# Squaring the expert activations on GpSimd instead of ScalarE in a fused attention and expert kernel

## The chip, the cores and the metric

The kernel runs on one core of a Trainium2 chip. The core's engines are PE (TensorE, matrix products and transposes), DVE (VectorE), ACT (ScalarE), POOL (GpSimd) and SP (SyncE, here only DMA). Each has its own instruction queue, works through it in order, and waits on semaphores that the others raise. The metric is the device time in microseconds of one execution; lower is better.

## The reference

The input is 2048 rows of 256 numbers, all float32. After a layer norm two layers read the same rows, and their outputs are added to x. The first has windowed attention and a fast-weight memory that goes from chunk to chunk (128 rows). The second is a mixture of 32 experts, of which 8 count for each row, and a shared expert. The change touches the experts; the memory matters because the rest of each chunk waits for it.

```python
def relu2(x): return jnp.square(jax.nn.relu(x))
x_lat = x @ fc1_w.T                                   # 128 wide
h = relu2(jnp.einsum('tl,eil->eti', x_lat, w1))       # 32 experts of 128
h = h * cw.T[:, :, None]
y_lat = jnp.einsum('eti,eli->tl', h, w2)
routed = y_lat @ fc2_w.T
shared = relu2(x @ shared_up_w.T) @ shared_down_w.T
...
# memory, per chunk, for each of W0, W1, W2 of four heads
for a, b, c in NS_COEFFS:                             # five steps
    A = X @ X.transpose(0, 2, 1)
    B = b * A + c * (A @ A)
    X = a * X + B @ X
W = (W + X) / (norm_of_rows(W + X) + 1e-05) * n
```

## The kernel before, in words

There are 16 chunks of 128 rows. `body(i, last)` is one round and is written out once per engine. A round finishes chunk i and prepares chunk m = i + 1. Fifteen rounds are alike and the last is shorter, since nothing follows. The order on each engine is written by hand: the five Newton-Schulz steps have four stages each (stages 0 to 19), for two groups g of heads whose buffers carry the group's number, and `fill` says what else stands behind each stage.

A stage of the memory goes as follows. PE transposes X (`ns_turn`), ACT copies the result to XT (`xt`), PE forms the gram products (`ns_gram`), DVE copies them to Am (`ns_a`), PE squares Am (`ns_pair`), DVE forms Mp (`ns_m`), PE multiplies by X, and DVE adds aX (`ns_x`), which POOL has computed from X and a_tile (`ax`). After the last step DVE updates Wn, sums its rows, POOL takes the roots (`row_pow`), DVE scales Wn (`renorm`), PE transposes it (`turn_w`) and ACT copies it to WT (`w_T`). Then comes the k side of the next round: products of WT on PE, copies `ks` on ACT, products kt, hid, dhb and dga on DVE with one (`k_u`) on POOL, and the gradients on PE (`grads`). A gradient norm follows, whose powers are on POOL (`ss_pow`).

The experts are done in eight blocks of four (u = 0 to 7). `h_up` on PE writes one 128x512 block to the PSUM bank HB. `h_relu` on ACT copies it with a relu into one of four buffers hq, then squares that buffer in place. `y_down` on PE reads hq and writes the bank YB. `y_acc` on DVE (or `y_first` on ACT for block 0) scales it by the routing weight and adds it into acc. HB is free again when the relu is done. Blocks 0 and 1 of a chunk are computed at the end of the round before. `shared_sq` on POOL squares the shared expert's block, of the same size, once a round.

In each round ACT's squares stand in its queue at these places: block 0 before the copy yT, 1 before the WT copies, 2 before the shared relu, 3 before the first XT copies, 4 before the copies of the query output, 5 before the sigmoids sgs, the third pair of XT copies and the square sq of the q and k heads, 6 before a table load, 7 before a logarithm and the copy prT.

Of the kernel before, what the change touches and what calls it, by code (L numbers as in the profile page):

```python
# [27 lines left out]
ALU = mybir.AluOpType  # L28
ACT = mybir.ActivationFunctionType
# [3 lines left out]
P = 128  # L33
# [12 lines left out]
EU = 4  # L46
NU = E // EU
# [26 lines left out]
def build(nc, x, wall_d, rows_d, wo, fast_d, affine_d, fc1T, fc2T, e1T, e2T, upT, downT, ident_d, fixed_d, out):  # L74
# [3 lines left out]
    with ExitStack() as ctx:  # L78
        def sb(name, shape):
            return ctx.enter_context(nc.sbuf_tensor(name, shape, F32))  # L80

        def bank(name):
            return ctx.enter_context(nc.psum_tensor(name, [P, 512], F32))

        def sem(name):
            return ctx.enter_context(nc.semaphore(name))
# [9 lines left out]
        e2_s = sb("e2_s", [P, E, P])  # L96
# [89 lines left out]
        xlT = sb("xlT", [P, P])  # L186
        ur = sb("ur", [P, SC, P])
        us = sb("us", [P, SC, P])
        hq = [sb(f"hq{b}", [P, EU, P]) for b in range(4)]
        acc = sb("acc", [P, EU, P])  # L190
        ya = sb("ya", [P, 2, P])
        ys = sb("ys", [P, P])
# [8 lines left out]
        HB = bank("HB")  # L201
        YB = bank("YB")
# [29 lines left out]
        e_h, e_hr, e_hq, e_y, e_acc = (sem(n) for n in ("h", "h_relu", "h_sq", "y", "acc"))  # L232
# [41 lines left out]
        @block.gpsimd  # L274
        def _(pool):

            win_scores = Expect(pool, e_as, "win_scores", first=2)
            win_pv = Expect(pool, e_av, "win_pv", first=2)
            win_raw = Expect(pool, e_rawv, "win_raw", first=3)
            win_vw = Expect(pool, e_win, "win_vw", first=5, step=2)  # L280
            pool.wait_ge(e_init, 1)

            def power(dst, src, expo, n):
                return pool.tensor_tensor(dst, src, expo[:, 0:n], ALU.pow)  # L284

            def prep_rstd(m):
                pool.wait_ge(e_veps, m + 1)
                power(rstd[:, 0:1], rstd[:, 1:2], neghalf, 1).then_inc(e_rstd, 1)

            def prep_n8(m):  # L290
                pool.wait_ge(e_ss8, m + 1)
                power(r8[:, 1, :], r8[:, 0, :], half, 8).then_inc(e_n8, 1)

            def prep_kl(m):

                pool.wait_ge(e_lr, m + 1)
                for g in range(G):
                    pool.wait_ge(e_dw[g], m)
                kk = qkn[:, D:2 * D].rearrange("p (h c) -> p h c", c=HD)
                vv = sl[:, 2 * D:3 * D].rearrange("p (h c) -> p h c", c=HD)  # L300
                for dst, src, n in ((kl0, kk, 0), (kl2, kk, 2), (vl1, vv, 1)):
                    ins = pool.tensor_tensor(dst[:, :, :], src, lr[:, :, n:n + 1].to_broadcast([P, NH, HD]), ALU.mult)
                ins.then_inc(e_kl, 1)

            def window(m, known):

                if known:
                    pool.wait_ge(e_as, m)
                    pool.wait_ge(e_av, m)
                    pool.wait_ge(e_rawv, m + 1)  # L310
                else:
                    win_scores.wait()
                    win_pv.wait()
                    win_raw.wait()
                pool.tensor_copy(akT[:, :, 0, :], akT[:, :, 1, :])
                pool.tensor_copy(vw[:, 0, :], vw[:, 1, :]).then_inc(e_win, 1)

                if known:
                    pool.wait_ge(e_win, 2 * m + 1)
                else:  # L320
                    win_vw.wait()
                pool.tensor_copy(vw[:, 1, :], raw[:, 2 * D:3 * D]).then_inc(e_win, 1)

            def restore_mask():

                pool.wait_ge(e_sm, 1)
                pool.wait_ge(e_later, 16 * NLATER)
                pool.tensor_copy(mask[:, 0, :], mask_prev[:, :]).then_inc(e_mask, 1)

            def k_u(i, g):  # L330
                pool.wait_ge(e_kc[g], i + 1)
                pool.tensor_tensor(kt[g][:, 3, :], ks[g][:, 1, :], ks[g][:, 2, :], ALU.mult).then_inc(e_ku[g], 1)

            def ss_pow(i, g):
                pool.wait_ge(e_sst[g], 3 * i + 1)
                power(r3[g][:, 2, :], r3[g][:, 1, :], half, 3).then_inc(e_pw[g], 1)

            def ax(i, g, it):
                pool.wait_ge(e_x[g], (NI + 1) * i + it + 1)
                pool.tensor_tensor(aX[g][:, :, :].rearrange("p w c -> p (w c)"),  # L340
                                   X[g][:, :, :].rearrange("p w c -> p (w c)"), a_tile[:, it, :],
                                   ALU.mult).then_inc(e_ax[g], 1)

            def row_pow(m, g):

                pool.wait_ge(e_rn[g], m + 1)
                power(r3[g][:, 4, :], r3[g][:, 3, :], half, 3).then_inc(e_rp[g], 1)

            def rms_pow(i):
                pool.wait_ge(e_msq, 2 * i + 2)  # L350
                power(r4[:, 1, :], r4[:, 0, :], neghalf, 4).then_inc(e_rms, 1)

            def shared_sq(i):
                pool.wait_ge(e_ur, i + 1)
                pool.tensor_tensor(us[:, :, :], ur[:, :, :], ur[:, :, :], ALU.mult).then_inc(e_us, 1)

            def body(i, last):
                if last:
                    shared_sq(i)
                    rms_pow(i)  # L360
                    return
                m = i + 1
                first = i == 0
                k_u(i, 0)
                k_u(i, 1)
                for g in range(G):
                    ss_pow(i, g)
                prep_rstd(m)
                fill = {0: [lambda: shared_sq(i)], 3: [lambda: rms_pow(i)],
                        9: [lambda: prep_n8(m)], 16: [lambda: window(m, first)],  # L370
                        17: [lambda: prep_kl(m)]}
                if first:
                    fill[13] = [restore_mask]
                for st in range(4 * NI):
                    if st % 4 == 0:
                        for g in range(G):
                            ax(i, g, st // 4)
                    for f in fill.get(st, []):
                        f()
                for g in range(G):  # L380
                    row_pow(m, g)

            prep_rstd(0)
            for g in range(G):
                row_pow(0, g)
            prep_n8(0)
            window(0, True)
            prep_kl(0)

            body(0, False)  # L390
            for i in range(1, LAST):
                body(i, False)
            body(LAST, True)


        @block.scalar
        def _(act):
# [9 lines left out]
            def a(out_, in_, func, **kw):  # L407
                return nc.scalar.activation(out_, in_, func, **kw)  # L408
# [78 lines left out]
                a(ur[:, :, :].rearrange("p s t -> p (s t)"), M0[:, :], ACT.Relu).then_inc(e_ur, 1)  # L487

            def h_relu(i, u):
                n = NU * i + u  # L490
                flat = hq[n % 4][:, :, :].rearrange("p s t -> p (s t)")
                act.wait_ge(e_h, n + 1)
                if n >= 4:
                    act.wait_ge(e_y, n - 3)
                a(flat, HB[:, :], ACT.Relu).then_inc(e_hr, 1)
                act.wait_ge(e_hr, n + 1)
                a(flat, flat, ACT.Square).then_inc(e_hq, 1)

            def y_first(i):

# [102 lines left out]
        def _(pe):  # L603
# [10 lines left out]
            def mm(out_, lhsT, rhs, start=True, stop=True):  # L614
                return pe.matmul(out_, lhsT, rhs, start=start, stop=stop)  # L615
# [203 lines left out]
            def y_down(i, u):  # L819
                pe.wait_ge(e_hq, NU * i + u + 1)  # L820
                pe.wait_ge(e_acc, NU * i + u)
                for e in range(EU):
                    ins = mm(YB[:, e * P:(e + 1) * P], hq[(NU * i + u) % 4][:, e, :], e2_s[:, EU * u + e, :])
                ins.then_inc(e_y, 1)

            def turn_y(i, last):
# [127 lines left out]
        def _(dve):  # L954
# [165 lines left out]
            def ns_m(i, g, it):  # L1120

                _, b, c = NS[it]
                dve.wait_ge(e_prod[g], 3 * NI * i + 3 * it + 2)
                nc.vector.scalar_tensor_tensor(Mp[g][:, :, :].rearrange("p w c -> p (w c)"),  # L1124
                                               Am[g][:, :, :].rearrange("p w c -> p (w c)"), b / c, CA[g][:, 0:3 * HD],
                                               ALU.mult, ALU.add).then_inc(e_mp[g], 1)
# [313 lines left out]
```

## Time and profile before

| | |
|---|---|
| median of three runs | 824.2 us (823.67 to 824.67) |
| the profiled execution | 823.67 us |
| its span, first to last instruction | 821.6 us |
| granted TensorE clock, mean | 0.996 of full speed |
| busy: PE, DVE, ACT, POOL | 773.3, 658.4, 429.5, 276.4 us |
| squares on ACT | 128, of 630 ns |
| aX products on POOL | 150, of 658 ns |

The profile gives, for each engine, the time in which its instructions ran. Matrix products are pipelined, so that a busy PE isn't PE at its peak. The idle time of an engine counts only where another one, or the end, depends on it; the waits and the timeline show that. Weight loads (PEld) overlap the products.

### The profile page before, as it was taken

Reading aid. Unit: us, or ns where it says so; the run is one execution under the profiler, and the core shown is the slowest. Engines: PE = TensorE matmul, PEld = TensorE weight load, DVE = VectorE, ACT = ScalarE, POOL = GpSimd, SP = SyncE. Lnnn points to the kernel's source line nnn. Section 1 sums busy time; section 2 is a strip of 40 time slices with the busy share of each in tenths; the row PEclk is TensorE's granted clock in tenths of the full one; section 3 lists DMA queues with packets and bytes.
Section 4 is the critical chain, followed back from the end, with each engine's and each line's share of the span. In section 5 each row is a group of like instructions: output and inputs, shape, how many; then the busy total and the mean of one; then the engine's idle time right before and its main releaser. Section 6 shows DMA issues by size and latency. Waiting matters only on the chain.

```text
span 821.6 us, 24761 instructions
## 1 busy us (share of the span) xinstructions
PE 773.3 (94%) x9776; PEld 668.8 (81%) x9776; DVE 658.4 (80%) x2592; ACT 429.5 (52%) x996; POOL 276.4 (34%) x407
## 2 busy tenths in 40 slices
PE   3899999999999999999999999999999999999997
PEld 1878888788887888878888788887888888788886
DVE  4778788887878879888698886978879788797865
ACT  2655455454555545555545555455555554545544
POOL 1433333334333343333433334333343323433220
PEclk9899999999999999999999999999999999999999
DMA  8100000000000000000000000000000000000000
GB/s 322 57 2 15 8 2 21 3 14 8 2 21 2 14 9 2 21 2 15 8 3 20 2 15 8 3 21 2 15 8 2 21 2 15 8 2 15 2 15 7
DMA packets 9810, 15.08 MB, mean 18 GB/s; under 512 B 1120, under 2 KB 8928, under 8 KB 9440
## 3 DMA queue, kind: packets, MB, share of 16 engines
q1 hardware_dynamic: 7904, 7.80, 3.1%
q10 hardware_dynamic: 1792, 5.70, 1.8%
q8 instruction: 78, 1.28, 0.7%
q14 instruction: 36, 0.29, 0.1%
HBM read 11.41 MB, written 2.10 MB: 16 GB/s over the span
## 4 chain that ended last, share of the span: by engine, by line
PE 75%; ACT 15%; DVE 5%; issue 4%; DMA 1%; SPq 0%; DVEq 0%
PE CC L615 24%; PE M L615 21%; PE HB L615 13%; PE YB L615 10%; ACT hq L408 6%; DVE acc L1314 2%; ACT L556 2%; ACT XT L408 2%; DVE Am L1117 2%; DMA rows<-in_rows 1%; PE M L773 1%; ACT prT L408 1%; ACT WT L408 1%; ACT sq L408 1%; PE CC L686 1%
## 5 line engine op out<-in xcount | busy, mean ns | idle before, releaser
L340 POOL TENSOR_TENSOR aX<-X,a_tile 128x192 f32<-128x192 f32 x150 | 95.6, 658 | 177.0 <-DVE X L1132 177.0
L615 PE MATMUL YB<-e_s,hq 128*128 128x128 f32 x1024 | 141.2, 281 | 5.9 <-DVE acc L1314 5.9
L615 PE MATMUL HB<-xlT,e_s 128*128 128x128 f32 x1024 | 142.9, 283 | 0.4 <-ACT xlT L408 0.4
L408 ACT ACTIVATE hq<-HB 128x512 f32<-128x512 f32 x128 | 76.4, 597 | 121.5 <-PE HB L615 121.5
L1314 DVE SCALAR_TENSOR_TENSOR acc<-YB,cw,acc 128x128 f32<-128x128 f32 x448 | 125.5, 342 | 15.0 <-PE YB L615 15.0
L284 POOL TENSOR_TENSOR r<-r,half 128x3 f32<-128x3 f32 (+1 forms) x78 | 77.9, 1011 | 171.9 <-DVE r L1102 71.3
L615 PEld LDWEIGHTS YB<-e_s,hq 128*128 128x128 f32 x1024 | 124.2, 191 | 11.7 <-issue 8.5
L615 PEld LDWEIGHTS HB<-xlT,e_s 128*128 128x128 f32 x1024 | 126.6, 193 | 6.9 <-ACT xlT L408 0.7
L408 ACT ACTIVATE hq<-hq 128x512 f32<-128x512 f32 x128 | 80.7, 630 | 4.0
L615 PEld LDWEIGHTS CC<-Am 64*64 64x64 f32 x1800 | 60.3, 134 | 20.6 <-DVE Am L1117 15.2
L615 PE MATMUL CC<-Am 64*64 64x64 f32 x1800 | 72.6, 222 | 1.8
L408 ACT ACTIVATE XT<-CC 128x256 f32<-128x256 f32 x150 | 48.7, 376 | 46.3 <-PE CC L686 46.1
L615 PEld LDWEIGHTS CC<-X,Mp 64*64 64x64 f32 x1800 | 58.3, 134 | 15.5 <-issue 9.0
L615 PE MATMUL CC<-X,Mp 64*64 64x64 f32 x1800 | 68.6, 222 | 0.0
L1132 DVE SCALAR_TENSOR_TENSOR X<-CC,aX 128x192 f32<-128x192 f32 x150 | 51.2, 350 | 20.7 <-PE CC L615 20.6
L1117 DVE COPY Am<-CC 128x192 f32<-128x192 f32 x150 | 48.6, 349 | 22.2 <-PE CC L615 20.6
L615 PEld LDWEIGHTS CC<-XT 64*64 64x64 f32 x1800 | 43.2, 133 | 28.1 <-ACT XT L408 26.0
L615 PE MATMUL CC<-XT 64*64 64x64 f32 x1800 | 55.5, 232 | 5.7 <-ACT XT L408 5.7
L615 PE MATMUL M<-wall,xnT 128*128 128x512 f32 (+1 forms) x128 | 56.7, 549 | 3.6 <-DMA rows<-in_rows 3.6
L1124 DVE SCALAR_TENSOR_TENSOR Mp<-Am,CC 128x192 f32<-128x192 f32 x150 | 49.8, 349 | 5.3 <-PE CC L615 4.8
L408 ACT ACTIVATE sig<-M 128x512 f32<-128x512 f32 (+1 forms) x32 | 15.7, 490 | 53.9 <-PE M L615 53.8
L284 POOL TENSOR_TENSOR r<-r,neghalf 128x4 f32<-128x4 f32 x16 | 16.2, 1015 | 71.6 <-DVE r L1187 71.6
(180 smaller groups left out, 1487.8 us busy)
## 6 DMA issues: line engine op xcount, KB each, us to landing
xa<-in_x SPq DMA_DIRECT2D x16, 128.0 KB, 2.1
e_s<-in_e1T ACTq DMA_DIRECT2D x1, 2048.0 KB, 12.8
e_s<-in_e2T ACTq DMA_DIRECT2D x1, 2048.0 KB, 19.5
xr<-in_x SPq DMA_DIRECT2D x16, 128.0 KB, 2.2
out<-ot SPq DMA_DIRECT2D x16, 128.0 KB, 1.7
wall<-in_wall SPq DMA_DIRECT2D x1, 820.0 KB, 7.0
up_s<-in_upT ACTq DMA_DIRECT2D x1, 512.0 KB, 15.5
down_s<-in_downT ACTq DMA_DIRECT2D x1, 512.0 KB, 19.5
```

The lines of the kernel that those rows point to most:

```text
L284: return pool.tensor_tensor(dst, src, expo[:, 0:n], ALU.pow)
L340: pool.tensor_tensor(aX[g][:, :, :].rearrange("p w c -> p (w c)"), X[g][:, :, :].rearrange("p w c -> p (w c)"), a_tile[:, it, :], ALU.mult ...
L408: return nc.scalar.activation(out_, in_, func, **kw)
L556: act.preload_act_table_set("sigmoid_and_others")
L615: return pe.matmul(out_, lhsT, rhs, start=start, stop=stop)
L686: pe.transpose(CA[g][:, P:2 * P], X[g][:, 1:3, :].rearrange("p w c -> p (w c)"), ident[:, :])\
L773: ins = pe.transpose(M1[:, n * P:(n + 1) * P], pr[:, h, w, :], ident[:, :])
L1117: nc.vector.tensor_copy(Am[g][:, :, :], CC[g][:, 0:6 * P].rearrange("p (w c) -> p w c", w=3)[:, :, 0:HD])\
L1124: nc.vector.scalar_tensor_tensor(Mp[g][:, :, :].rearrange("p w c -> p (w c)"), Am[g][:, :, :].rearrange("p w c -> p (w c)"), b / c, CA[g][ ...
L1132: nc.vector.scalar_tensor_tensor(X[g][:, :, :].rearrange("p w c -> p (w c)"), CB[g][:, 0:3 * HD], NS[it][2], aX[g][:, :, :].rearrange("p w ...
L1314: ins = nc.vector.scalar_tensor_tensor(acc[:, e, :], y, w, acc[:, e, :], ALU.mult, ALU.add)
```

## The change

The two halves of `h_relu` are taken apart. ACT only does the relu, from HB into one of two new buffers hr. POOL does the square as a product of hr with itself, into one of two buffers hq (four before). The POOL instruction `h_sq(i, u)` waits for the relu of its block and for `y_down` of the block two before it; the relu waits for the square of the block two before it. `h_sq` is put into POOL's queue at eight places of a round.

```diff
-        hq = [sb(f"hq{b}", [P, EU, P]) for b in range(4)]
+        hr = [sb(f"hr{b}", [P, EU, P]) for b in range(2)]
+        hq = [sb(f"hq{b}", [P, EU, P]) for b in range(2)]
...
+            def h_sq(i, u):
+                pool.wait_ge(e_hr, NU * i + u + 1)
+                if u > 1 or not (isinstance(i, int) and i == 0):
+                    pool.wait_ge(e_y, NU * i + u - 1)
+                b = u % 2
+                pool.tensor_tensor(hq[b][:, :, :], hr[b][:, :, :], hr[b][:, :, :], ALU.mult).then_inc(e_hq, 1)
...
             def h_relu(i, u):
-                n = NU * i + u
-                flat = hq[n % 4][:, :, :].rearrange("p s t -> p (s t)")
-                act.wait_ge(e_h, n + 1)
-                if n >= 4:
-                    act.wait_ge(e_y, n - 3)
-                a(flat, HB[:, :], ACT.Relu).then_inc(e_hr, 1)
-                act.wait_ge(e_hr, n + 1)
-                a(flat, flat, ACT.Square).then_inc(e_hq, 1)
+                act.wait_ge(e_h, NU * i + u + 1)
+                if u > 1 or not (isinstance(i, int) and i == 0):
+                    act.wait_ge(e_hq, NU * i + u - 1)
+                a(hr[u % 2][:, :, :].rearrange("p s t -> p (s t)"), HB[:, :], ACT.Relu).then_inc(e_hr, 1)
...
-                    ins = mm(YB[:, e * P:(e + 1) * P], hq[(NU * i + u) % 4][:, e, :], e2_s[:, EU * u + e, :])
+                    ins = mm(YB[:, e * P:(e + 1) * P], hq[u % 2][:, e, :], e2_s[:, EU * u + e, :])
```

On POOL, from the roots of the row sums at a round's end (r30, r31 with half) to the first aX of the next round, before:

```order
L284 TENSOR_TENSOR r30<-r30,half 128x3
L284 TENSOR_TENSOR r31<-r31,half 128x3
L332 TENSOR_TENSOR kt0<-ks0 128x128
L332 TENSOR_TENSOR kt1<-ks1 128x128
L284 TENSOR_TENSOR r30<-r30,half 128x3
L284 TENSOR_TENSOR r31<-r31,half 128x3
L284 TENSOR_TENSOR rstd<-rstd,neghalf 128x1
L340 TENSOR_TENSOR aX0<-X0,a_tile 128x192
```

and with the change:

```order
L285 TENSOR_TENSOR r31<-r31,half 128x3
L363 TENSOR_TENSOR hq0<-hr0 128x512
L333 TENSOR_TENSOR kt0<-ks0 128x128
L333 TENSOR_TENSOR kt1<-ks1 128x128
L363 TENSOR_TENSOR hq1<-hr1 128x512
L285 TENSOR_TENSOR r30<-r30,half 128x3
L285 TENSOR_TENSOR r31<-r31,half 128x3
L285 TENSOR_TENSOR rstd<-rstd,neghalf 128x1
L363 TENSOR_TENSOR hq0<-hr0 128x512
L341 TENSOR_TENSOR aX0<-X0,a_tile 128x192
```

Square 0 stands between the roots and the k side's product, square 1 between that and the powers of the gradient norm, square 2 before the first aX. Further on POOL, from the power of r8 (stage 9) to the last aX pair of the round, with the change (before, the same without the three squares):

```order
L285 TENSOR_TENSOR r8<-r8,half 128x8
L363 TENSOR_TENSOR hq1<-hr1 128x512
L341 TENSOR_TENSOR aX0<-X0,a_tile 128x192
L341 TENSOR_TENSOR aX1<-X1,a_tile 128x192
L363 TENSOR_TENSOR hq0<-hr0 128x512
L363 TENSOR_TENSOR hq1<-hr1 128x512
```

These are squares 5, 6 and 7. Squares 3 and 4 stand behind the shared expert's square and behind the second aX pair. On ACT, at the end of a round (yT is the turned expert sum, WT the turned fast weights), before:

```order
L408 ACTIVATE hq0<-hq0 128x512
L408 ACTIVATE yT<-M1 128x128
L408 ACTIVATE hq1<-HB 128x512
L408 ACTIVATE hq1<-hq1 128x512
L408 ACTIVATE WT0<-CC0 64x3x64 x2
L408 ACTIVATE WT1<-CC1 64x3x64 x2
```

and with the change:

```order
L426 ACTIVATE hr0<-HB 128x512
L426 ACTIVATE yT<-M1 128x128
L426 ACTIVATE hr1<-HB 128x512
L426 ACTIVATE WT0<-CC0 64x3x64 x2
L426 ACTIVATE WT1<-CC1 64x3x64 x2
```

The WT copies follow the relu of block 1 directly. At the other seven places the square is gone in the same way.

## Rows read from the trace of the kernel before

**Rows 1.** The page, part 1: busy us of each engine (share of span).
```profile
PE 773.3 (94%) x9776; PEld 668.8 (81%) x9776; DVE 658.4 (80%) x2592; ACT 429.5 (52%) x996; POOL 276.4 (34%) x407
```
**Rows 2.** Waits: who waited for whom; us in total, times, longest us.
```profile
PE CC L615 <- ACT WT L408: 12.3, 14, 0.9
```
**Rows 3.** Groups by form: xcount, busy us, mean ns, idle before and releaser.
```profile
L408 ACT ACTIVATE hq<-hq 128x512 f32<-128x512 f32 x128 | 80.7, 630 | 4.0
...
L355 POOL TENSOR_TENSOR us<-ur 128x512 f32<-128x512 f32 x16 | 16.6, 1035 | 9.7 <-ACT ur L408 9.7
```
**Rows 4.** One line, the xn scaling: duration min/median/max in ns.
```profile
L987 DVE TENSOR_SCALAR xn<-xa,mv,rstd x16: 414/683/687, 5.9 to 751.4; 128x256 f32<-128x256 f32 x16
```
**Rows 5.** Timeline, k side: start, us, engine, line, operation [idle before <-releaser].
```profile
438.07 0.46 POOL L332 TENSOR_TENSOR kt<-ks 128x128 f32<-128x128 f32 x1 [0.22 <-ACT ks L408]
...
438.32 0.36 DVE L1069 TENSOR_TENSOR kt<-ks,kt 128x128 f32<-128x128 f32 x1
438.60 0.28 DVE L1080 TENSOR_TENSOR dhb<-kt,ks 128x128 f32<-128x128 f32 x1
...
439.81 0.28 DVE L1074 TENSOR_TENSOR dga<-kt 128x128 f32<-128x128 f32 x1
...
439.56 0.33 PE L615 MATMUL CC<-kl,dga 128*64 128x64 f32 x2
...
440.14 0.33 PE L615 MATMUL CC<-kl,dga 128*64 128x64 f32 x2
```
**Rows 6.** Timeline, end of a round: POOL, DVE, ACT, PE, and DVE's k side.
```profile
431.08 1.67 POOL L284 TENSOR_TENSOR r<-r,half 128x3 f32<-128x3 f32 x2 [3.23 <-DVE r L1142]
...
432.38 0.76 DVE L1161 TENSOR_SCALAR Wn<-Wn,r,nrm 128x64 f32<-128x64 f32 x3
...
435.05 1.32 ACT L408 ACTIVATE WT<-CC 64x192 f32<-64x192 f32 x4
...
435.83 0.67 PE L615 MATMUL CC<-WT,qkT 128*128 128x256 f32 x2 [0.90 <-ACT WT L408]
...
437.35 0.29 DVE L1061 TENSOR_TENSOR kt<-CC,ks 128x128 f32<-128x128 f32 x1 [1.06 <-ACT ks L408]
```
**Rows 7.** Timeline, first stages of a round: ACT, PE, POOL.
```profile
446.29 0.64 ACT L408 ACTIVATE XT<-CC 128x256 f32<-128x256 f32 x2
...
446.22 0.27 PE L686 MATMUL CC<-ident,X 128*128 128x128 f32 x1
446.71 0.46 PE L615 MATMUL CC<-XT 64*64 64x64 f32 x12 [0.22 <-ACT XT L408]
...
445.42 1.36 POOL L340 TENSOR_TENSOR aX<-X,a_tile 128x192 f32<-128x192 f32 x2
```
**Rows 8.** Timeline, middle of a round: ACT and PE.
```profile
409.81 0.64 ACT L408 ACTIVATE XT<-CC 128x256 f32<-128x256 f32 x2
...
410.27 0.69 PE L615 MATMUL CC<-XT 64*64 64x64 f32 x24
...
413.39 1.13 PE L615 MATMUL YB<-e_s,hq 128*128 128x128 f32 x8 [0.33 <-DVE acc L1314]
```
**Rows 9.** Timeline, stages 11 to 15: POOL, DVE, PE.
```profile
415.60 1.14 POOL L340 TENSOR_TENSOR aX<-X,a_tile 128x192 f32<-128x192 f32 x2 [2.21 <-DVE X L1132]
...
414.05 0.17 DVE L1030 SCALAR_TENSOR_TENSOR lt<-z 128x12 f32<-128x12 f32 x1
...
417.11 0.15 DVE L1258 TENSOR_TENSOR gs<-g 128x4 f32<-128x4 f32 x1
...
420.50 0.34 DVE L1124 SCALAR_TENSOR_TENSOR Mp<-Am,CC 128x192 f32<-128x192 f32 x1
...
420.90 0.92 PE L615 MATMUL CC<-X,Mp 64*64 64x64 f32 x24
```
**Rows 10.** Timeline, block 7: its relu on ACT, its y_down on PE.
```profile
420.98 0.60 ACT L408 ACTIVATE hq<-HB 128x512 f32<-128x512 f32 x1 [0.30 <-PE HB L615]
...
425.44 1.16 PE L615 MATMUL YB<-e_s,hq 128*128 128x128 f32 x8
```

More of the change, by code:

```diff
@@ L355, in shared_sq @@
                 pool.tensor_tensor(us[:, :, :], ur[:, :, :], ur[:, :, :], ALU.mult).then_inc(e_us, 1)
+            def h_sq(i, u):
[4 more added lines that the diff above has]
+                pool.tensor_tensor(hq[b][:, :, :], hr[b][:, :, :], hr[b][:, :, :], ALU.mult).then_inc(e_hq, 1)
             def body(i, last):
                 if last:
+                    h_sq(i, 1)
+                    h_sq(i, 2)
                     shared_sq(i)
+                    h_sq(i, 3)
                     rms_pow(i)
+                    for u in range(4, NU):
+                        h_sq(i, u)
                     return
@@ L365, in body @@
                 k_u(i, 1)
+                h_sq(i, 1)
                 for g in range(G):
@@ L368, in body @@
                 prep_rstd(m)
-                fill = {0: [lambda: shared_sq(i)], 3: [lambda: rms_pow(i)],
-                        9: [lambda: prep_n8(m)], 16: [lambda: window(m, first)],
+                h_sq(i, 2)
+                fill = {0: [lambda: shared_sq(i)], 1: [lambda: h_sq(i, 3)], 3: [lambda: rms_pow(i)],
+                        4: [lambda: h_sq(i, 4)], 9: [lambda: prep_n8(m), lambda: h_sq(i, 5)],
+                        12: [lambda: h_sq(i, 6)], 14: [lambda: h_sq(i, 7)], 16: [lambda: window(m, first)],
                         17: [lambda: prep_kl(m)]}
@@ L381, in body @@
                     row_pow(m, g)
+                h_sq(m, 0)
             prep_rstd(0)
@@ L388, in _ @@
             prep_kl(0)
+            h_sq(0, 0)
             body(0, False)
```

## The prediction

> **What bounds the kernel now.** I read the page's busy times first. PE is busy for 773.3 of 821.6 us, and ACT for only 429.5 and POOL for 276.4 [rows 1]. So neither ACT nor POOL is short of time. What counts is whether one of their instructions stands in front of something that PE or the vector engine waits for. The list of waits names one such place outright: PE waits 12.3 us in all for the transposed weights that ACT copies, 14 times, 0.9 us at most [rows 2]. I then read one whole round (one chunk of 128 rows, 15 such rounds and a shorter last one) engine by engine in the timeline, asking at each of the eight squares what is queued behind it. All times below are of that round; the others repeat its pattern.
>
> **What is taken from ACT.** A square costs ACT 630 ns [rows 3], and there are eight in a round. Five of them stand before nothing that is late (ACT is idle soon after). Three stand on the path:
> - *Weights.* The square of h block 1 of the next chunk ends where the WT copies start, at 435.05; they take 1.32 us in all, and PE starts the k side at 435.83, after 0.90 us of idleness [rows 6]. Without the square the copies start 0.55 us earlier (the relu before it must still end). PE is free by then, so its start moves by 0.55.
> - *First XT copies.* They start at 446.29, behind a square; PE starts the gram products at 446.71, though its last transpose before them started at 446.22 and a transpose takes 0.11 of the queue [rows 7]. So PE could start at 446.33: gain 0.38.
> - *Middle of the round.* The XT copies at 409.81 stand behind a square and a small sigmoid, and the 128x512 square of the q and k heads behind them. PE's gram products start at 410.27, and its y_down at 413.39 waits 0.33 us for DVE's accumulation [rows 8], whose chain on DVE begins with the sum over that q/k square of ACT. With the 0.63 gone from ACT (of which 0.09 was overlap with its neighbours) it all comes 0.54 us earlier: 413.39 becomes 412.85.
>
> With nothing lost elsewhere that is 0.55 + 0.38 + 0.54 = 1.47 us a round, 22 us over 15 rounds.
>
> **What is put on POOL.** Eight multiplies of 128x512 with both inputs in SBUF. The trace has the same instruction once a round, the shared experts' square, at 1035 ns [rows 3]: 8.3 us more for POOL in a round of 51. I checked each against its reader, y_down. The tightest is block 7: its relu starts at 420.98 and takes 0.60, so its POOL square ends near 422.7, and y_down reads it at 425.44 [rows 10]. PE's other work hides the latency there and, with more room, at the other seven. The relus need an hr buffer whose square two blocks earlier is long done. The powers and aX products that follow a square on POOL start up to 1.04 us later: the first aX pair is read 5 us later, and the powers of the gradient norms and of rms wait for DVE far longer than that. I put all of this at zero. If that cover were gone (a square directly before a power that DVE waits for) each would cost up to 1.04.
>
> **What the squares do to DVE.** This is the term that decides. DVE instructions with two SBUF inputs are longer when POOL runs. So are copies and scalings from SBUF to SBUF: the xn scaling takes 414 ns at its fastest and 683 at the median [rows 4], and in the rounds the long ones lie over POOL's aX. Instructions that take one input from PSUM show no such growth. How long POOL holds them off can be read at the k side: POOL's product from 438.07 lasts 0.46 and ends at 438.53; DVE's product from 438.32 takes 0.36 where the next takes 0.28 [rows 5]. So it ran from 438.40, that is 0.13 before POOL's end. A 1.04 us square then blocks DVE for about 0.9 us from its start. Since a queued POOL instruction starts about 0.04 before the end of the one before it (two aX of 0.59 take 1.14 [rows 9]), I can place each square.
>
> - *Square 1, behind k_u.* It starts at 438.49 and blocks until 439.4. DVE has there a row of products with two SBUF inputs, from dhb at 438.60 to the second dga at 439.81 [rows 5]. dhb moves to 439.4, and both dga by 0.80. PE takes up the gradients at 439.56 and 440.14, right when dga are ready (439.28, 440.09) [rows 5]: no slack. Cost 0.80. The lower bound is 0, if DVE, whose instructions overlap by 0.08, keeps the port through the row. Against that stands the first aX at 445.42: the pair takes 1.36 instead of 1.14 [rows 7, 9], it waited for one DVE product and then got in ahead of xn, which is blocked. I take 0.80.
> - *Square 0, behind the row powers.* These end at 432.75 [rows 6], and the square blocks until 433.6. DVE's three scalings of Wn start at 432.38 and take 0.76 [rows 6]; the third is held 0.7. The second group's Wn, its transposes and WT copies follow 0.7 later, and so does the vector work up to the k side. The vector engine then reaches it at 437.02 instead of 437.35 [rows 6], a gain of 0.33 instead of 0.55. If scalings of 64 columns don't need the port the 0.55 stands.
> - *Square 2, before the first aX.* xn is blocked by 0.4 more, and DVE's Am copies behind it by the same. The second Am waits for PE in any case. The 0.38 stands.
> - *Squares 5 and 6.* Square 5 follows the r8 power and overlaps a small product from 414.05 [rows 9]: 0.2. Square 6 starts at 416.70 behind aX (which ends at 416.74) and blocks until 417.6; DVE's sum of group scores at 417.11 [rows 9] is held some 0.4 (DVE has moved forward by then). From there to the Mp at 420.50 DVE is without a gap, and Mp ends at 420.84, 0.06 before PE needs it at 420.90 [rows 9]. So the 0.54 gained in the middle of the round becomes 0.54 - 0.2 - 0.41 = -0.07, within what reaches PE.
> - *Squares 3, 4, 7.* 3 meets only instructions with a PSUM input. 4 delays the norm of q by 0.6, against an idle time of DVE over 1 us before X. 7 delays lr by 0.5, and DVE waits for PE soon after. Zero.
>
> **The sum.** 0.33 - 0.80 + 0.38 - 0.07 = -0.16 us a round (a loss), 15 rounds: 2.4 us. The shorter last round has other work around the squares; I put it at zero, with 0.5 either way. The profiled execution took 823.67 us, 2.07 of it outside its span of 821.6, which gives 826.1. The median of the three runs is 0.5 above that execution, so I say 826.5.
>
> *A rule against the change.* The Trainium skill, page "SBUF — State Buffer", section "Who interferes with whom", says that GpSimd and DVE instructions with two SBUF inputs share one port pair under an exclusive lock, held for the whole instruction. The trace agrees that one blocks the other, but shows DVE free again about 0.13 us before POOL's end. By the page's rule to the letter, three blocking squares cost 0.13 more each, 5.9 us over 15 rounds. That would be 832.4, inside rival 3.
>
> **Rivals.**
> 1. *DVE keeps the port.* If a queued square can't get in between overlapping DVE products, square 1 runs after them, costs nothing, and the round gains 0.33 + 0.38 - 0.07 = 0.64: 9.6 us, 814.6. For it: the products follow each other with no idle time. Against: the first aX, as above. It decides from the point where the delay of the second dga falls under 0.64 us, since from there the round gains.
> 2. *No collision matters* (the queues shift apart, or DVE makes up in gaps): 1.47 a round, 802. Against it: xn is long at the median of 16 [rows 4].
> 3. *The blocks are longer or more.* Each of squares 0, 1, 6 holds DVE to its end, and square 4 or 7 has a cost too, about 0.55 a round more: 8.2 us, 834.7. For it: DVE is gapless from 411 to 421, where any delay reaches PE. Against it: the 0.13 at 438.53.
> 4. *The gains are not PE's.* ACT is early but PE finds the next wait at once; only square 1 costs: 0.80 x 15 = 12, 836.
>
> **Chances.** The forecast has 0.50, with its own range 821 to 831: 0.34 of it slower, 0.12 within 0.2%, 0.04 faster. Rival 1 has 0.21 and rival 2 0.06, faster. Rivals 3 and 4 have 0.15 and 0.04, slower. The rest, 0.04, is the same within what can be told. 0.2% is 1.6 us, about what a measurement of this kernel can tell from no change. That gives faster 0.31, same 0.16, slower 0.53. For 8 in 10 the range must take in rival 1's time and rival 3's: 812 to 835.
>
> **What would show it.** After the change PE's idle time for WT should fall from 0.90 to under 0.2 us a round, with some 0.2 to 0.5 of waiting for Wn in its place; the second dga should end 0.8 us later behind the first silu product than now (2.74 us); dhb should be about 1 us long over a square. The first gram product should follow the transposes at once. A short dhb, and a square on POOL longer than 1.6 us at the same place, would mean rival 1. A faster kernel with a long dhb would mean that I have misjudged the slack at the gradients.

## The result, and the profile after

The changed kernel took 831.2 us (median of four runs, 830.2 to 831.5) against 823.9 for the kernel before beside it: a ratio of 1.009, with a 95% interval of 1.007 to 1.0108. It is slower by 0.9%. The forecast was slower, 826.5 within 812 to 835. The measured time lies in that range and just outside the narrower 821 to 831 that the forecast gave itself. The direction and the mechanism held; the loss came out at 7.3 us where 2.4 was worked out.

The busy times, in the page of the changed kernel (answers to [rows 1]):

```profile
span 828.1 us, 24889 instructions
...
PE 780.7 (94%) x9776; PEld 668.5 (81%) x9776; DVE 714.6 (86%) x2592; ACT 354.0 (43%) x868; POOL 406.8 (49%) x535
```

ACT has 75.5 us less. POOL has 130 more. DVE executes the same 2592 instructions, yet it is busy for 714.6 us where it was 658.4: 56 us of waiting, counted inside its instructions. Six groups grew by 59 us in all (their instructions overlap a little): dhb by 12.7, the scalings of Wn by 11.5, one scaling of lt by 10.9, the first product for the norm of q by 9.6, gs by 7.5 and xn by 6.7. Each of the lengthened instructions lies over a square on POOL. The groups by form for POOL show the squares, 1071 ns on average where the one of [rows 3] takes 1035:

```profile
L363 POOL TENSOR_TENSOR hq<-hr 128x512 f32<-128x512 f32 x128 | 137.1, 1071 | 71.9 <-ACT hr L426 71.9
```

PE's lists of waits (us in total, times, longest; the last line is of its weight loads) answer to [rows 2]:

```profile
PE CC L629 <- DVE dga L1088: 10.5, 15, 1.5
PE CC L629 <- DVE Mp L1138: 7.6, 15, 0.5
...
PE CC L629 <- ACT WT L426: 2.6, 14, 0.2
...
PEld CC L736 <- DVE Wn L1175: 12.9, 30, 1.3
```

The wait for WT fell from 12.3 us to 2.6, which is what taking a square away from ACT was to do. Two others took its place, 18.1 us together: PE's wait for dga, which occurred once before (1.3 us) and now in each of the 15 rounds, and PE's wait for Mp, which the list of before doesn't have. The weight loads wait for Wn twice in each round, 0.86 us a round in all, where it was 0.4 us once in the whole kernel. All three are waits for DVE, which no line of the change touches.

The timeline of the changed kernel at the k side of a round, DVE then POOL then PE (start, us, engine, line, operation, idle before and releaser; answers to [rows 5]):

```profile
441.26 0.44 DVE L1083 TENSOR_TENSOR kt<-ks,kt 128x128 f32<-128x128 f32 x1
441.62 1.12 DVE L1094 TENSOR_TENSOR dhb<-kt,ks 128x128 f32<-128x128 f32 x1
...
441.10 0.45 POOL L333 TENSOR_TENSOR kt<-ks 128x128 f32<-128x128 f32 x1 [0.59 <-ACT ks L426]
441.52 1.08 POOL L363 TENSOR_TENSOR hq<-hr 128x512 f32<-128x512 f32 x1
...
443.30 0.30 PE L629 MATMUL CC<-kl,dga 128*64 128x64 f32 x2 [0.64 <-DVE dga L1088]
```

dhb takes 1.12 us where it took 0.28. POOL's square 1 stands behind the product from 441.10 and ends at 442.60, dhb at 442.74. PE is idle for 0.64 us before the gradients.

### The profile page after: what moved, and what is told of

It is laid out like the page before. It is cut to its first block, busy times and chain, and to the rows that moved or that the text cites. A ratio compares the mean times of both kernels' runs of the same rounds, so it can differ in the third digit from the quotient of the medians.

```text
span 828.1 us, 24889 instructions
## 1 busy us (share of the span) xinstructions
PE 780.7 (94%) x9776; PEld 668.5 (81%) x9776; DVE 714.6 (86%) x2592; ACT 354.0 (43%) x868; POOL 406.8 (49%) x535
## 4 chain that ended last, share of the span: by engine, by line
PE 53%; DVE 33%; issue 6%; ACT 5%; POOL 2%; DMA 1%; SPq 0%; DVEq 0%
PE CC L629 18%; PE M L629 13%; PE HB L629 8%; DVE acc L1328 8%; PE YB L629 8%; DVE Wn L1175 4%; DVE Mp L1138 2%; DVE dhb L1094 2%; DVE X L1146 2%; PE CC L699 2%; DVE Am L1131 2%; POOL r L285 2%; DVE sm L1233 1%; DMA rows<-in_rows 1%; PE CC L700 1%
## 5 line engine op out<-in xcount | busy, mean ns | idle before, releaser
L363 POOL TENSOR_TENSOR hq<-hr 128x512 f32<-128x512 f32 x128 | 137.1, 1071 | 71.9 <-ACT hr L426 71.9
L341 POOL TENSOR_TENSOR aX<-X,a_tile 128x192 f32<-128x192 f32 x150 | 92.9, 640 | 79.9 <-DVE X L1146 79.9
L426 ACT ACTIVATE hr<-HB 128x512 f32<-128x512 f32 x128 | 76.1, 594 | 128.5 <-PE HB L629 128.5
L426 ACT ACTIVATE XT<-CC 128x256 f32<-128x256 f32 x150 | 50.8, 381 | 59.7 <-PE CC L700 59.5
L629 PE MATMUL CC<-Am 64*64 64x64 f32 x1800 | 69.8, 223 | 1.9
L1146 DVE SCALAR_TENSOR_TENSOR X<-CC,aX 128x192 f32<-128x192 f32 x150 | 51.3, 352 | 13.4 <-PE CC L629 13.3
L629 PEld LDWEIGHTS CC<-XT 64*64 64x64 f32 x1800 | 43.2, 133 | 20.7 <-ACT XT L426 14.7
L699 PE MATMUL CC<-ident,X 128*64 128x128 f32 x150 | 39.7, 281 | 0.0
L333 POOL TENSOR_TENSOR kt<-ks 128x128 f32<-128x128 f32 x30 | 13.7, 459 | 51.0 <-ACT ks L426 51.0
## 6 DMA issues: line engine op xcount, KB each, us to landing
e_s<-in_e1T ACTq DMA_DIRECT2D x1, 2048.0 KB, 12.7
```

The source lines that it names most:

```text
L363: pool.tensor_tensor(hq[b][:, :, :], hr[b][:, :, :], hr[b][:, :, :], ALU.mult).then_inc(e_hq, 1)
L699: pe.transpose(CA[g][0:HD, 0:P], X[g][:, 0, :], ident[:, :])
L1146: nc.vector.scalar_tensor_tensor(X[g][:, :, :].rearrange("p w c -> p (w c)"), CB[g][:, 0:3 * HD], NS[it][2], aX[g][:, :, :].rearrange("p w ...
```

## Where the round changed

I took the same PE instructions in a middle round of both traces and compared the time between them. A round lasts 50.97 us before and 51.35 after.

| from, to (on PE) | change, us | forecast |
|---|---|---|
| h_up of block 1 to the k side of the second group | -0.15 | -0.33 |
| to the second group's gradients (square 1) | +0.84 | +0.80 |
| to the first gram product | -0.29 | -0.38 |
| to y_down of block 4 | -0.67 | -0.54 |
| to the last product of step 4 (squares 5, 6) | +0.72 | +0.61 |
| to the next h_up of block 1 | -0.07 | 0 |
| sum | +0.38 | +0.16 |

Fifteen rounds of 0.38 are 5.7 us. After the last full round (counted from its end's first WT copy) the changed kernel needs 30.79 us to the end instead of 29.62, so 1.2 us more. The spans differ by 6.5. (The medians differ by 7.3: the profiled execution of the changed kernel, 830.14 us, was its shortest.)

## The experiments

Each kernel ran beside the kernel before (820.9 to 825.1 us in these runs). Each time is a median. The cuts show the lines that matter; semaphore counts that follow from them are left out.

**The squares left out.** In the kernel before, the relu writes hq, and nothing squares; the experts' sum is another number.

```diff
                 a(flat, HB[:, :], ACT.Relu).then_inc(e_hr, 1)
-                act.wait_ge(e_hr, n + 1)
-                a(flat, flat, ACT.Square).then_inc(e_hq, 1)
...
-                pe.wait_ge(e_hq, NU * i + u + 1)
+                pe.wait_ge(e_hr, NU * i + u + 1)
```

> The kernel before with the squares left out altogether (relu only, so the experts' sum is another number): no square on ACT, none on POOL. It measures the whole gain on ACT. My theory: the squares cost 0.57 a round before the weight copies, 0.3 to 0.4 before the first XT copies and 0.55 to 0.67 in the middle of a round, so about 1.5 us a round, 22 us: 802 us. Rival (the gains are not PE's, another wait stands right behind): under 5 us, 819 or more.

Measured: 799.1 us, a ratio of 0.970 (0.9675 to 0.9724); a round lasts 49.36 us, 1.61 less. So the gain on ACT was real and PE could take it up. By the same marks on PE as in the table, the k side's stretch is shorter by 0.66, the one to the first gram product by 0.29 and the one to y_down of block 4 by 0.66 (the forecast's gains were 0.55, 0.38 and 0.54); the other three are within 0.01 of before. Rival 4 of the forecast falls. The changed kernel had these 1.6 us a round in hand and gave back more.

**One POOL product more, that nobody waits for.** In the kernel before, with the squares on ACT. dm is a new pair of tiles that DVE fills once at the start:

```diff
                 k_u(i, 1)
+                pool.tensor_tensor(dm[1][:, :, :], dm[0][:, :, :], dm[0][:, :, :], ALU.mult)
```

> The kernel before, with one more POOL instruction a round behind k_u: a 128x512 product of an unused tile with itself, which nobody waits for. Port theory: it holds off DVE's products with two SBUF inputs by 0.84 us, dhb is 1.1 us long in place of 0.28, and the kernel loses 0.84 x 15 = 12.6 us: 836.5 us. Rival (what the changed kernel loses there is the later arrival of the square or of the next power on POOL, not the port): nobody reads this product and the next power waits 4 us for DVE anyway, so 824 us.

Measured: 837.2 us, 1.0165 (1.0138 to 1.0192), 12.8 us more. DVE's timeline of that run (start, us, engine, line, operation):

```profile
447.46 0.36 DVE L1072 TENSOR_TENSOR kt<-ks,kt 128x128 f32<-128x128 f32 x1
447.74 1.12 DVE L1083 TENSOR_TENSOR dhb<-kt,ks 128x128 f32<-128x128 f32 x1
448.79 0.28 DVE L1068 SCALAR_TENSOR_TENSOR kt<-ks,kt 128x128 f32<-128x128 f32 x1
```

The same 1.12 us, at the same instruction. 0.84 x 15 = 12.6. No reader of the product exists, so the later arrival of a result can't be the cause.

**The same place, an instruction that only writes.**

```diff
                 k_u(i, 1)
+                pool.memset(dmw[:, :], 1.0)
```

> The same as the run before, but the POOL instruction at that place only writes: a memset of 128x1024, which should last about as long. If it is the read side of the port that DVE's second input needs, DVE isn't held off: dhb stays at 0.28 us and the kernel at 824 us. If any POOL instruction blocks DVE there, 830 us or more, as with the product.

Measured: 823.8 us, 0.9999 (0.9987 to 1.001). The group of the memset on POOL (count, busy us, mean ns, idle before), and the line of DVE's dhb (min/median/max in ns):

```profile
L368 POOL MEMSET dmw<- 128x1024 f32 x15 | 14.3, 953 | 0.0
```
```profile
L1084 DVE TENSOR_TENSOR dhb<-kt,ks x30: 277/279/281, 30.6 to 745.3; 128x128 f32<-128x128 f32 x30
```

POOL is busy for 953 ns at that place, against 1088 for the product, and no dhb is longer than 281 ns. So it isn't enough that POOL is busy or writes there. The product reads SBUF and the memset doesn't.

**The same product, another place.** Behind the shared experts' square:

```diff
-                fill = {0: [lambda: shared_sq(i)], 3: [lambda: rms_pow(i)],
+                fill = {0: [lambda: shared_sq(i), lambda: pool.tensor_tensor(dm[1][:, :, :], dm[0][:, :, :], dm[0][:, :, :], ALU.mult)], 3: [lambda: rms_pow(i)],
```

> The kernel before with the same extra POOL product of 128x512 a round as in the run that lost 13 us, but behind the shared experts' square, where DVE has instructions with a PSUM input. Port theory: nothing of DVE is held, 824 us. Rival (a POOL product of this size costs wherever it stands, through POOL's load or the memory): 830 or more.

Measured: 824.2 us, 1.0 (0.999 to 1.001). The work is that of the run that lost 12.8 us, and it costs nothing here. That alone doesn't show that DVE's PSUM inputs are spared, because DVE has little to do in that stretch (timeline of this run, POOL then DVE):

```profile
447.67 1.04 POOL L356 TENSOR_TENSOR us<-ur 128x512 f32<-128x512 f32 x1
448.67 1.04 POOL L370 TENSOR_TENSOR dm<-dm 128x512 f32<-128x512 f32 x1
...
448.14 0.40 DVE L1212 TENSOR_SCALAR akT<-M,affine 128x128 f32<-128x128 f32 x1
448.46 0.34 DVE L1119 COPY Am<-CC 128x192 f32<-128x192 f32 x1
449.61 0.36 DVE L1119 COPY Am<-CC 128x192 f32<-128x192 f32 x1 [0.81 <-PE CC L616]
```

Of the product's 1.04 us DVE is idle for 0.81, waiting for PE. What speaks for the PSUM inputs are the rows beside the shared square: akT (from the PSUM bank M) takes 0.40 us and Am (from CC) 0.34, as elsewhere.

**Square 1 alone undone.** In the changed kernel, block 1 is squared on ACT, behind y_first; the other seven squares stay on POOL. sq1 is the square on ACT, from hr into hq.

```diff
                 k_u(i, 1)
-                h_sq(i, 1)
...
                 y_first(i)
+                sq1(i)
                 h_relu(i, 2)
```

> The changed kernel with square 1 alone undone: it is on ACT behind the first block's accumulation, the other seven stay on POOL. Port theory: dhb is 0.28 us long, 0.84 a round is gone, and in the last round the second hold of the Wn scalings (0.7 to 1.1) too: 14 us less than the changed kernel, 817 us. Rival (square 0, 2 or the whole POOL load costs as much as square 1): 825 or more.

Measured: 816.5 us, 0.9909 (0.9895 to 0.9924). Against the changed kernel's 831.2 that is 14.7 us less. By the traces a round is 0.85 shorter (50.50 against 51.35) and the last one 0.7, together 13.5, and the spans differ by 13.4. dhb is never over 280 ns (its line in that run, min/median/max in ns):

```profile
L1111 DVE TENSOR_TENSOR dhb<-kt,ks x30: 275/278/280, 30.5 to 738.9; 128x128 f32<-128x128 f32 x30
```

**Square 0 moved as well.** The kernel of the last run, with square 0 behind a wait for DVE's W1BD of the second group.

```diff
+                pool.wait_ge(e_bd[1], m + 1)
                 h_sq(m, 0)
```

> As the run with square 1 on ACT, with square 0 moved too: on POOL, but behind W1BD of the second group. It measures square 0 by itself. In the changed kernel the second group's WT copies and the k side products that read them stand 0.42 us later against the first group's than before. If that is square 0's block of a Wn scaling, it goes: 0.42 x 15 = 6.3 us less than with square 1 on ACT, 810 us. If square 0 now blocks cw and with it DVE's way to the k side, or if the second group's lateness was hidden, 815 or more.

Measured: 809.6 us, 0.983 (0.9816 to 0.9845): 6.9 less than with square 1 on ACT alone. One line of the list of waits of the two runs, without and with the move (us in total, times, longest):

```profile
PEld CC L750 <- DVE Wn L1192: 12.2, 30, 0.6
```
```profile
PEld CC L751 <- DVE Wn L1193: 0.4, 1, 0.4
```

A round lasts 50.03 us instead of 50.50. So square 0 by itself costs 0.47 us a round by the traces, 0.46 by the times.

**Squares 0 and 1 both moved, all eight on POOL.** Square 1 moves in the last round too.

```diff
                 k_u(i, 1)
-                h_sq(i, 1)
...
+                pool.wait_ge(e_bd[1], m + 1)
                 h_sq(m, 0)
+                h_sq(m, 1)
```

> The changed kernel with squares 0 and 1 moved: both stand together behind a wait for W1BD of the second group, after DVE's scalings of Wn and before k_u. The same eight squares on POOL, but off DVE's k side products and Wn scalings. Port theory: the 0.84 of square 1 is gone, the second group's weights come 0.42 earlier, PE's k side follows by 0.57 instead of 0.15: 1.26 us a round less than the changed kernel, and the last round's 1.1 less too, 20 us: 811 us. Rival (POOL's load or latency as such is what costs): unchanged at 830, or slower, since k_u now waits up to 0.2 us for the two squares.

Measured: 816.7 us, 0.9917 (0.9891 to 0.9943). It is 14.5 us less than the changed kernel, and I had expected 20. The last round's part came as expected (29.66 us from the last WT copies, as before). The rest went to a new collision: the two squares follow each other until 2.7 us after the first WT copy. The first holds cw (0.55 longer). POOL's two k_u products, which wait behind the second square, then come one behind the other while DVE has its first k side products, and hold two of them (0.23 and 0.27 longer):

```profile
432.90 0.92 POOL L333 TENSOR_TENSOR kt<-ks 128x128 f32<-128x128 f32 x2
...
432.95 0.56 DVE L1080 SCALAR_TENSOR_TENSOR kt<-ks,kt 128x128 f32<-128x128 f32 x1
433.43 0.55 DVE L1092 TENSOR_TENSOR hid<-kt,ks 128x128 f32<-128x128 f32 x1
```

The squares end at 432.95, where kt starts. The second dga comes 0.49 later against the copies than before. There is room for one square at this place, not for two.

**Square 6 moved.**

```diff
-                        12: [lambda: h_sq(i, 6)], 14: [lambda: h_sq(i, 7)], 16: [lambda: window(m, first)],
+                        12: [lambda: pool.wait_ge(e_rt, 13 * m + 3), lambda: h_sq(i, 6)], 14: [lambda: h_sq(i, 7)], 16: [lambda: window(m, first)],
```

> The changed kernel with one wait more: square 6 on POOL also waits until DVE has done the sum of group scores (gs), so that it runs beside instructions with a PSUM input. Port theory: gs is no longer 0.5 us longer and DVE reaches Mp 0.5 us earlier, 0.55 a round less at PE: 8 us, 823 against 831 of the changed kernel. Rival (that stretch has slack after all, or its gain is swallowed by the table load behind prT): 829 to 831.

Measured: 823.2 us, 0.9991 (0.9981 to 1.0), 8.0 less than the changed kernel. The sum of group scores, in the changed kernel and in this one (min/median/max in ns):

```profile
L1272 DVE TENSOR_TENSOR gs<-g x16: 165/653/662, 20.5 to 779.3; 128x4 f32<-128x4 f32 x16
```
```profile
L1272 DVE TENSOR_TENSOR gs<-g x16: 151/153/166, 20.8 to 772.8; 128x4 f32<-128x4 f32 x16
```

An instruction on four elements per partition was held for 0.5 us in each round and cost the kernel 1% (a round lasts 50.85 us instead of 51.35). A single wait in POOL's queue brings the changed kernel back to the time before.

**Both moves together.** The edits of the last two kernels in one: squares 0 and 1 behind W1BD, square 6 behind the wait for the group scores.

> Squares 0 and 1 behind W1BD and square 6 behind gs, together. If the two collisions are separate terms, their gains add: 816.7 (squares 0 and 1 moved) less 8 = 809 us. If the first gain has already moved DVE off the second collision, 815 or more.

Measured: 809.2 us, 0.9817 (0.9801 to 0.9834): the two gains add to within 1 us.

**All squares on ACT, three of them at other places.** POOL has none. h_only is the relu of a block and h_sq its square, both on ACT; h_relu is the two together.

```diff
                 y_first(i)
+                h_sq(i, 1)
                 h_relu(i, 2)
...
-                h_relu(i, 3)
-                fill = {1: [lambda: h_relu(i, 4)], 2: [lambda: q_out(i), lambda: prep_xnT(m)],
+                h_only(i, 3)
+                fill = {0: [lambda: h_sq(i, 3)], 1: [lambda: h_relu(i, 4)], 2: [lambda: q_out(i), lambda: prep_xnT(m)],
...
-                        8: [lambda: prep_sq8(m)], 9: [lambda: prep_vT(m), lambda: h_relu(i, 6), to_exp],
+                        8: [lambda: prep_sq8(m)], 9: [lambda: prep_vT(m), lambda: h_sq(i, 5), lambda: h_relu(i, 6), to_exp],
...
-                h_relu(m, 1)
+                h_only(m, 1)
```

> No square on POOL: the kernel before with its eight squares on ACT, of which three stand elsewhere in ACT's queue. Square 1 goes behind the first block's accumulation instead of before the WT copies, square 3 behind the first XT copies, square 5 behind the copy of vT. If it was the place of three squares on ACT that cost, and not ACT's load, this takes nearly all that leaving the squares out brought (799.1 us), less a rest where a moved square meets the next copy: 801 us. Rival (the moved squares arrive late for y_down, or a copy behind the new place is late): 812 or more.

Measured: 799.6 us, 0.9703 (0.9689 to 0.9718). This is 24 us less than the kernel before, and as fast as with no squares at all (799.1; a round lasts 49.35 and 49.36 us). So the five squares that stayed where they were cost nothing that can be told, as the forecast had said. ACT's timeline at the end of a round of this kernel:

```profile
420.68 0.60 ACT L408 ACTIVATE hq<-HB 128x512 f32<-128x512 f32 x1 [0.44 <-PE HB L624]
421.18 1.33 ACT L408 ACTIVATE WT<-CC 64x192 f32<-64x192 f32 x4
422.89 1.23 ACT L408 ACTIVATE ks<-CC 128x128 f32<-128x128 f32 x4 [0.39 <-PE CC L624]
...
425.80 1.14 ACT L408 ACTIVATE acc<-YB,cw 128x128 f32<-128x128 f32 x4 [0.95 <-PE YB L624]
426.82 0.65 ACT L408 ACTIVATE hq<-hq 128x512 f32<-128x512 f32 x1
428.13 0.60 ACT L408 ACTIVATE hq<-HB 128x512 f32<-128x512 f32 x1 [0.67 <-PE HB L624]
```

The WT copies follow the relu directly. The square stands behind acc, and ACT is idle for 0.67 us after it even so. The change had moved eight squares to another engine in order to shift three of them in time.

## Why the prediction was right, and where it was not

**The direction and the deciding term.** Square 1 was sized at 0.80 from one pair of rows, the 0.36 and 0.28 of [rows 5], and it is 0.84 both in the changed kernel and with an idle product in its place. That POOL gets in between overlapping DVE instructions, read from xn and the first aX, held. Rival 1 (814.6) falls with it. Rival 2 falls with the long dhb and gs. [rows 5] don't show quite what the forecast read for the gradients: the first dga ends 0.28 us before PE takes it up, behind y_down. Only the second, 0.05 before, has no slack, and it is the one that sets the stretch. The page of the Trainium skill, "SBUF — State Buffer", section "Who interferes with whom", limits the conflict of a DVE instruction with two SBUF inputs to GpSimd instructions that read SBUF. The memset run agrees: 953 ns of POOL, and dhb at 279. The same section says that the port is held for the whole instruction. The trace doesn't bear that out to the letter. dhb runs for its last 0.28 us from 442.47, and square 1 ends at 442.60: 0.13 before the end, as in [rows 5]. The hold is 0.84 and not 0.80 because the square itself took 1.08 and not 1.04; one that lasted to its end would be 0.97. So the time by the page's rule, 832.4, lies near the measured 831.2 by coincidence.

**The middle of the round.** Forecast -0.54 + 0.61 = +0.07, measured -0.67 + 0.72 = +0.05. Each is 0.1 larger than sized, and they cancel, which is luck. The whole square came through as gain (0.66 with no squares at all), not the 0.54 left after an overlap. On the other side square 5 held lt for 0.22 (0.2 forecast) and square 6 held gs for 0.50 (0.41). That this gain would be eaten again was the step I was least sure of; the move of square 6 shows it by itself (8.0 us, and 0.50 a round in the traces, where 0.55 was expected).

**The k side of the second group: the step that failed first.** I gave this stretch -0.33 and it measured -0.15, 2.7 us over 15 rounds. Square 0 did hold the third scaling of Wn as said (1.48 us for the three in place of 0.76). What was wrong is what followed, in the timeline of the changed kernel (DVE, ACT, PE):

```profile
435.57 1.48 DVE L1175 TENSOR_SCALAR Wn<-Wn,r,nrm 128x64 f32<-128x64 f32 x3
...
437.66 0.66 ACT L426 ACTIVATE WT<-CC 64x192 f32<-64x192 f32 x2
438.74 0.66 ACT L426 ACTIVATE WT<-CC 64x192 f32<-64x192 f32 x2 [0.42 <-PE CC L736]
...
439.55 0.67 PE L629 MATMUL CC<-WT,qkT 128*128 128x256 f32 x2 [0.18 <-ACT WT L426]
```

In [rows 6] the four WT copies are one run of 1.32 us. Now the second pair waits 0.42 us for PE's transposes of the second group, ends at 439.40, and PE takes it up 0.15 later. I had sized the lateness from the first silu product on DVE, which belongs to the first group. The second group's path is the later one, and it is the one the gradients wait for. Moving square 0 gave back 6.9 us, so the term is 0.46 and not 0.22 (0.55 less 0.33). The gain beside it was too small as well, 0.66 without squares where I took 0.55, so that the stretch is off by less than the hold. One of the forecast's own signs says the same: the second dga ends 3.85 us behind the first silu product, 1.11 later than before, where 0.8 was named.

**The first gram product.** -0.29 for -0.38, 1.3 us over the rounds. I let PE follow its own last transpose after 0.11; it follows after 0.20. With no squares at all that distance is 0.20 too, and the stretch is 0.29 shorter. So no square on POOL eats the rest, square 2 included; what PE does in those 0.09 stays open.

**The last round: set to zero, measured +1.2.** I had excused it with other work around the squares. In it nothing stands on POOL between squares 0 and 1, so square 1 starts as soon as its relu is done and meets the scalings of the second group (timeline of the changed kernel in the last round, DVE and then POOL):

```profile
794.99 1.49 DVE L1175 TENSOR_SCALAR Wn<-Wn,r,nrm 128x64 f32<-128x64 f32 x3
...
796.80 1.48 DVE L1175 TENSOR_SCALAR Wn<-Wn,r,nrm 128x64 f32<-128x64 f32 x3
```
```profile
795.33 1.10 POOL L363 TENSOR_TENSOR hq<-hr 128x512 f32<-128x512 f32 x1
797.17 1.06 POOL L363 TENSOR_TENSOR hq<-hr 128x512 f32<-128x512 f32 x1 [0.74 <-ACT hr L426]
```

Both groups are held here, each for 0.7 us. With square 1 on ACT 0.7 of the 1.2 is gone, and with both squares behind W1BD the last stretch takes 29.66 us again. The order of the last round stood in the source and could have been walked like the other; this was an omission, not a surprise.

**The zeros.** Squares 2, 3, 4 and 7 were put at nothing. xn is 0.45 us longer. By the means of DVE's groups, the first product for the norm of q (128x4) is 0.60 longer, from 153 to 755 ns, and the scaling of lt before lr 0.68, from 174 to 856. None of the three shows on PE by more than 0.1 us a round: the stretches in which they stand came out at -0.29 and -0.67, the latter as with no squares at all, and at -0.07.

The terms were off by 0.18 (k side of the second group), 0.09 (first gram product), 0.04 (square 1), -0.02 (middle) and -0.07 (the end of the round): 0.22 a round, 3.3 us over 15 rounds. With the last round's 1.2 that leads from the 2.4 forecast to 6.9, where the spans differ by 6.5.

**How near it was.** The forecast of 0.16 a round is a small rest of a gain of 1.47 and holds of 1.63. Measured, the gain is 1.61 (no squares at all) and the holds 1.99. Square 0's hold alone was 0.24 larger than sized; gains larger by as much, with the holds as sized, would have made the kernel faster. So the direction came out right partly by luck, and the forecast had given slower no more than 0.53. In time rival 3 (834.7) is nearer to 831.2 than the forecast. Of what it said, the holds were longer than sized, though none lasted to POOL's end, and squares 4 and 7 did lengthen an instruction of DVE each, but cost PE nothing that shows.

## What to carry to other kernels

An engine's load says little where every engine is below full. Ask of the instruction that you want to move what stands behind it in its queue, and try first to move it within the queue: here that gave 3%, where the other engine cost 0.9%. Before placing work on POOL that reads SBUF, list DVE's instructions of that stretch by where their inputs are. Those with two SBUF inputs, and scalings from SBUF to SBUF, stopped here until 0.13 to 0.26 us before POOL's instruction ended, however small they were. And walk each group and the odd last round to its own end; the later of two parallel paths is the one to size.

## What the runs showed of the hardware

The hold takes no note of size: a sum over four elements per partition took 653 ns for 153. A POOL memset of 953 ns at a place where a product of 1088 ns cost 12.8 us cost nothing. When the hold ends is the same from round to round. Take from the recorded end of a held instruction its length when it isn't held: in the changed kernel that point lies 0.13 us before the end of the square for dhb (15 times), gs (15) and the first product for the norm of q (15), 0.15 for the scaling of lt (128x12, 15 times), and 0.26 for the scalings of Wn (128x64, 16 times) and of xn (128x256, 15 times). POOL's own instruction grows too when it meets a DVE instruction already under way: square 2 starts at 449.29, 0.04 us after DVE's product for X (0.36 long, two SBUF inputs), and takes 1213 ns instead of 1035. DVE's next instruction, xn, then waits for it. Its line in the changed kernel (min/median/max in ns):

```profile
L1001 DVE TENSOR_SCALAR xn<-xa,mv,rstd x16: 412/1130/1131, 5.9 to 757.6; 128x256 f32<-128x256 f32 x16
```

xn is a scaling with one SBUF tensor as input, and it is held like the two-input products: 1.13 us for its 0.41.
